# Eight shared-expert units in the attention stage's last slots, and three sum tables instead of two

## The chip, the cores and the metric

One Trainium2 chip, one of its cores. The metric is the time of the program on the device in microseconds (us). Engines: PE is TensorE (PEld its weight loads), DVE is VectorE, ACT is ScalarE, POOL is GpSimd, SP is SyncE, which issues most DMAs.

## What is computed

4096 tokens (16 sequences of 256, width 256) pass four layers, each `x = layernorm(x + layer(x))`: a recurrent attention (rwkv), a feed-forward layer on quantized weights (ffn), a latent attention with 16 heads (mla), and a mixture of experts (moe). The last one matters here:

```python
slots_token, slots_w = ...                    # router: 4 of 32 experts for each token, 160 places each
Xp = x[slots_token].reshape(E, C, d)
Y = (silu(Xp @ W_gate) * (Xp @ W_up)) @ W_down        # for each expert
out = zeros.at[slots_token].add(Y * slots_w)
shared = silu(x @ shared_gate.T) * (x @ shared_up.T) @ shared_down.T
return out + shared
```

## The kernel before

The four layers run one after another, each in its own block with a barrier at its end. In each block every engine has its own in-order list of instructions, written out by hand, and semaphores tie the lists together. Each fp32 operand of a matmul is split into a high part (ACT) and a low part (DVE, the source minus the high part), and each product is three matmuls (`PARTS`).

**Attention stage** (`attention_phase`). All engines walk over slots (seq, v), v = 0 to 11, for seq = 0 to NSEQ + 2 (NSEQ is 16). A sequence's scores are taken in its own slots; its projections run one and two sequences ahead; its last output projection is at (seq + 1, 8), its layer norm at (seq + 1, 9) and (seq + 1, 11); its routing in the slots of seq + 2 and the first two of seq + 3. Routing is a chain of 28 small steps, counted by the semaphore `chain`, that go back and forth between DVE (`route`, with times in `ROUTE_AT`), POOL (`route_pool`) and PE (transposes, logits, places). At its end POOL's `scatter` sends the rows of x, in eight indirect DMAs per sequence in slots 2 to 9 of seq + 3, to the table `slots` in DRAM. After (16, 3) no scores or sums are left: slots (16, 4) to (18, 11) hold only the last projection and the routing of sequences 14 and 15. SP stores x3 and loads x rows.

**Mixture stage** (`moe_phase`). SP loads expert weights and the table's rows (`e_rows`), eight experts ahead. For each expert e: PE transposes its rows (`expert_turn`), ACT and DVE split them and the weights, PE makes gate and up (`expert_in`), ACT takes silu, DVE the product, ACT and DVE split it, PE makes y (`expert_out`), ACT scales y into `y_rows` (`copy_y`), and POOL's `add_rows` adds it with two indirect accumulating DMAs of 80 rows into two tables in DRAM, `sums[0]` and `sums[1]`; each waits for the DMA before it on the same table. The shared expert works on 16 units of 256 tokens: `turn_x`, `shared_gate`, `shared_up`, `shared_out` on PE with their splits on ACT and DVE, and `add_shared` on DVE, which puts x + shared into `total`. One unit is made before the expert loop, one is spread over every three experts (`PACE`), and the last four come after the loop. Then the close: for each unit SP loads the two tables' rows (`load_sums`, after all scatters have landed, four units ahead), POOL adds the first (`add_first`), DVE adds the second and takes statistics (`combine`), POOL raises the variance to -1/2 (`rsqrt`), DVE makes the shift, ACT applies the norm and issues the store. The tables are zeroed in the ffn stage (`zero_tables`, one piece of each for each of its eight blocks).

## Time and profile before

| | us |
|---|---|
| median of 3 runs | 2151.86 (2151.37 to 2152.52) |
| the profiled execution, its time | 2142.46 |
| its span (first to last instruction) | 2140.6 |

The page of the profile gives busy time and instructions of each engine over the span, and the span in 40 equal slices (53.5 us each), a digit for tenths of a slice:

```profile
PE 1916.3 (90%) x12560; PEld 1707.8 (80%) x12560; DVE 1565.7 (73%) x4293; ACT 1049.0 (49%) x2674; POOL 844.8 (39%) x877
...
PE   6999999999999869995899999999999999739880
...
DVE  7978877788777635553578888888888888636547
ACT  5443333433333223331477666666666667326543
POOL 1222222323233200000244565665665555635556
PEclk9999999999999979996899999999999999869995
DMA  3200000000000043435100110000000000046756
```

Slices 1 to 14 are rwkv, 15 to 19 ffn, 20 to 35 the latent attention, the rest the mixture. PEclk is the clock that TensorE was granted, in tenths of full speed. The chain that ended last is followed back from the last instruction and takes at each step what released it:

```profile
DMA sums<-moe_y_rows,moe_e_rows 5%; DVE moe_stats L2458 1%; PE moe_up_ps L2503 1%; PE moe_down_ps L2524 0%; DVE moe_total L2454 0%; DVE moe_var_eps L2466 0%; PE moe_gate_ps L2503 0%; DVE moe_hidden L2373 0%; DVE moe_moments L2463 0%; ACT moe_h_high L2264 0%; PE moe_xt L2490 0%; DVE moe_h_low L2378 0%; DMA moe_e_rows<-slots 0%; DMA moe_x_rows<-x 0%; ACT moe_x_out L2347 0%
```

### The profile page before, as it was taken

What the parts mean: (1) busy time and instruction counts of PE and PEld (TensorE: products, weight loads), DVE (VectorE), ACT (ScalarE), POOL (GpSimd) and SP (SyncE); (2) the same over time, 40 slices, a digit from 0 to 9 for tenths busy, and PEclk for the clock granted to TensorE, in tenths of its full rate; (3) what the DMA queues carried; (4) which work ended last, traced back from release to release, by engine and by line L of the source; (5) the groups of instructions that cost most, each with busy time, mean ns of one, the idle gap of its engine ahead of it and who ended that gap; (6) DMA issues with size and microseconds to landing.
All of it is one profiled execution on the core that took longest, in us unless ns stands there. A gap on an engine that the chain in (4) does not pass through costs nothing. (4 is left out here: it accounts for less than half of the span.)

```text
span 2140.6 us, 36853 instructions
## 1 busy us (share of the span) xinstructions
PE 1916.3 (90%) x12560; PEld 1707.8 (80%) x12560; DVE 1565.7 (73%) x4293; ACT 1049.0 (49%) x2674; POOL 844.8 (39%) x877
## 2 busy tenths in 40 slices
PE   6999999999999869995899999999999999739880
PEld 5788888888888758884799889888888889639780
DVE  7978877788777635553578888888888888636547
ACT  5443333433333223331477666666666667326543
POOL 1222222323233200000244565665665555635556
PEclk9999999999999979996899999999999999869995
DMA  3200000000000043435100110000000000046756
GB/s 118 79 8 23 23 9 30 1 30 21 11 20 1 20 133 127 127 117 181 43 11 16 35 33 19 20 19 19 17 17 19 23 17 12 13 142 146 167 107 217
DMA packets 100619, 117.25 MB, mean 55 GB/s; under 512 B 12392, under 2 KB 92332, under 8 KB 99793
## 3 DMA queue, kind: packets, MB, share of 16 engines
q1 hardware_dynamic: 83792, 102.59, 15.1%
q0 software_dynamic: 12288, 8.11, 2.7%
q10 hardware_dynamic: 4352, 4.20, 0.7%
q8 instruction: 102, 1.67, 0.3%
q14 instruction: 85, 0.69, 0.1%
HBM read 75.42 MB, written 55.53 MB: 61 GB/s over the span
## 5 line engine op out<-in xcount | busy, mean ns | idle before, releaser
L212 POOL TENSOR_TENSOR rwkv_gate<-rwkv_key,rwkv_gate 128x512 f32<-128x512 f32 x128 | 203.6, 1590 | 529.4 <-DVE rwkv_key L408 529.4
L1196 POOL TENSOR_TENSOR mla_w_raw<-mla_w_raw,mla_row_inv 128x512 f32<-128x512 f32 x192 | 199.2, 1038 | 313.3 <-DVE mla_row_inv L1558 311.9
L1370 ACT ACTIVATE mla_w_raw<-mla_w_raw,mla_least 128x256 f32<-128x256 f32 (+1 forms) x512 | 227.8, 446 | 100.4 <-DVE mla_least L1542 99.3
L279 ACT ACTIVATE rwkv_gate<-rwkv_r 128x512 f32<-128x512 f32 x128 | 76.6, 598 | 403.9 <-DVE rwkv_o_low L332 400.8
L1542 DVE CUSTOM_DVE_ANT_0 mla_w_raw<-mla_score,mla_mask 128x256 f32<-128x256 f32 (+1 forms) x512 | 156.7, 352 | 81.4 <-PE mla_score L1881 81.2
L393 DVE TENSOR_TENSOR rwkv_kv<-rwkv_v,rwkv_key 128x512 f32<-128x512 f32 x128 | 88.0, 688 | 126.1 <-PE rwkv_v L441 123.8
L400 DVE TENSOR_TENSOR_SCAN rwkv_state<-rwkv_decay_w,rwkv_kv 128x256 f32<-128x256 f32 x256 | 166.1, 691 | 4.1
L1881 PE MATMUL mla_score<-mla_k_high,mla_q_high 128*128 128x256 f32 (+1 forms) x512 | 155.7, 304 | 0.0
L458 PE MATMUL rwkv_out<-rwkv_w_high,rwkv_o_high 128*128 128x256 f32 x512 | 142.2, 278 | 5.5 <-DVE rwkv_o_low L332 5.5
L1881 PE MATMUL mla_score<-mla_k_high,mla_q_low 128*128 128x256 f32 (+1 forms) x512 | 143.7, 281 | 0.0
L1881 PE MATMUL mla_score<-mla_k_low,mla_q_high 128*128 128x256 f32 (+1 forms) x512 | 143.2, 280 | 0.0
L458 PE MATMUL rwkv_out<-rwkv_w_low,rwkv_o_high 128*128 128x256 f32 x512 | 141.9, 277 | 0.0
L458 PE MATMUL rwkv_out<-rwkv_w_high,rwkv_o_low 128*128 128x256 f32 x512 | 141.9, 277 | 0.0
L1282 POOL DMA_INDIRECT slots<-mla_x_out,mla_slot_now x128 | 129.0, 1008 | 32.2 <-issue 22.2
L1386 ACT ACTIVATE mla_p_high<-mla_turn 128x512 fp32r<-128x512 f32 x192 | 114.0, 594 | 48.4 <-PE mla_turn L1890 48.3
L1552 DVE TENSOR_TENSOR mla_p_low<-mla_turn,mla_p_high 128x512 fp32r<-128x512 f32 x192 | 127.9, 666 | 0.5 <-ACT mla_p_high L1386 0.5
L2214 POOL DMA_INDIRECT sums<-moe_y_rows,moe_e_rows x64 | 92.7, 1448 | 87.3 <-DMA sums<-moe_y_rows,moe_e_rows 48.7
L1890 PE MATMUL mla_turn<-mla_ident,mla_w_raw 128*128 128x128 f32 x768 | 116.6, 274 | 11.3 <-DVE mla_p_low L1552 11.3
L1890 PEld LDWEIGHTS mla_turn<-mla_ident,mla_w_raw 128*128 128x128 f32 x768 | 91.4, 141 | 35.7 <-issue 22.5
L1909 PE MATMUL mla_o<-mla_p_high,mla_v_high 128*128 128x256 f32 x384 | 117.2, 305 | 0.7 <-DVE mla_o_low L1563 0.4
L1332 ACT ACTIVATE mla_q_high<-mla_turn 128x512 fp32r<-128x512 f32 x128 | 76.4, 599 | 68.4 <-PE mla_turn L1858 68.2
L1909 PE MATMUL mla_o<-mla_p_high,mla_v_low 128*128 128x256 f32 x384 | 107.9, 281 | 0.0
(372 smaller groups left out, 6464.8 us busy)
## 6 DMA issues: line engine op xcount, KB each, us to landing
moe_w_raw<-in_experts SPq DMA_DIRECT2D x32, 384.0 KB, 4.6
rwkv_w_raw<-in_rkvo SPq DMA_DIRECT2D x16, 512.0 KB, 3.3
moe_y_in<-sums SPq DMA_DIRECT2D x32, 256.0 KB, 3.4
sums<-ffn_empty SPq DMA_DIRECT2D x14, 512.0 KB, 7.7
slots<-ffn_empty SPq DMA_DIRECT2D x8, 722.5 KB, 6.4
moe_e_rows<-slots SPq DMA_DIRECT2D x32, 180.6 KB, 2.8
mla_w_raw<-in_mla_heads SPq DMA_DIRECT2D x4, 1280.0 KB, 7.2
rwkv_x_in<-in_x_t SPq DMA_DIRECT2D x16, 256.0 KB, 3.1
```

Source lines behind the costliest of these rows:

```text
L212: nc.gpsimd.tensor_tensor(gate[:, c % 2, :], key[:, c % 2, :], gate[:, c % 2, :], ALU.mult).then_inc(gated_done, 1)
L400: last_scan = nc.vector.tensor_tensor_scan(out=state[:, q, 1:SEQ + 1], data0=decay_w[:, c:c + 1].to_broadcast([P, SEQ]), data1=kv[:, q * S ...
L458: last = nc.tensor.matmul(out_ps[j // 2][:, (j % 2) * D:(j % 2 + 1) * D], o_part[op][:, c % 2, j * P:(j + 1) * P], w_part[wp][:, c, 3 * D: ...
L1196: nc.gpsimd.tensor_tensor(unit, unit, row_inv[:, v % PR, 0:len(heads)].rearrange("p (h a) -> p h a", a=1) .to_broadcast([P, len(heads), ke ...
L1282: nc.gpsimd.indirect_dma_start(slots_dram, bass.IndirectOffsetOnAxis(slot_now[:, of % 2, i:i + 1], 0), x_out[:, of % 2, i // TOPK, :], Non ...
L1370: last = nc.scalar.activation(probs[:, v % PR, i * keys:(i + 1) * keys], masked[:, v % 2, i * keys:(i + 1) * keys], ACT.Exp, bias=least[:, ...
L1386: nc.scalar.activation(p_part[0][:, v % PR, :], turn_ps[n % TURN_BANKS][:, :], ACT.Copy)\
L1542: last = nc.vector.tensor_tensor_reduce(out=masked[:, v % 2, i * keys:(i + 1) * keys], in0=score_ps[v % 2][:, i * keys:(i + 1) * keys], in ...
L1552: nc.vector.tensor_tensor(p_part[1][:, v % PR, :], turn_ps[n % TURN_BANKS][:, :], p_part[0][:, v % PR, :].bitcast(F32), ALU.subtract).then ...
L1881: last = nc.tensor.matmul(score_ps[v % 2][:, i * keys:(i + 1) * keys], q_part[qp][:, tile, h * P:(h + 1) * P], k_part[kp][:, par, 0:keys], ...
L1890: last = nc.tensor.transpose(ps[:, i * P:(i + 1) * P], probs[:, v % PR, i * P:(i + 1) * P], ident[:, :])
L1909: last = nc.tensor.matmul(out, v_part[vp][:, seq % 2, kb, b, :], probs_t, start=(i == 0), stop=(i == len(terms) - 1))
```

## The change

Units 0 to 7 of the shared expert (`EARLY`) are made in `attention_phase`, the other eight (`LATE`) in `moe_phase`, one ahead of the expert loop and one for every three of its first 21 experts; none is left for after the loop. The shared weights are loaded at slot (15, 0) into a part of `w_raw` that is free by then, and split in slots (15, 8) to (15, 10). The first unit is transposed at (16, 2); then the work is cut into 17 half steps, each at a slot of the list `TAIL`: an even one makes the gate product of its unit and the down product and add of the unit before, an odd one transposes the next unit and makes this one's up product and hidden values. They stand in each engine's list behind what that slot held before. PSUM banks and buffers of the scores, sums and projections are used for it. x + shared of these units is kept in `q_rows`, the split weights in `wq_high`; both buffers now outlive the stage.

There are three sum tables (`SUMS`): scatter number 2e + a goes into table (2e + a) % 3 and waits for the scatter three before. All three are zeroed in the ffn stage and loaded in the close, where DVE makes two adds instead of one.

```diff
-SUMS = 2
+SUMS = 3
...
+UT = 2
+UNIT = UT * P
+UNITS = TOKENS // UNIT
+XRING = 4
+WS = 3 * KD * SI
+EARLY = 8
+WS_SLOT = 8
+FIRST_X = (NSEQ, 2)
+TAIL = [(NSEQ + s, v) for s, v in ((0, 4), (0, 6), (0, 7), (0, 9), (0, 10), (1, 0), (1, 1), (1, 3), (1, 4), (1, 6),
+                                   (1, 7), (1, 9), (1, 10), (2, 0), (2, 2), (2, 4), (2, 6))]
...
+def kept_total(q_rows, u):
+
+    flat = q_rows[:, :, :, :].rearrange("p a h c -> p (a h c)")
+    return flat[:, u * UT * D:(u + 1) * UT * D].rearrange("p (t d) -> p t d", d=D)
...
+        shared_flat = w_raw[:, :, :, :].rearrange("p a h c -> p (a h c)")
+        ws_raw = shared_weights_of(shared_flat[:, 0:WS])
+        gate, hidden = (shared_flat[:, at:at + SC * UNIT].rearrange("p (c t) -> p c t", c=SC)
+                        for at in (WS, 2048))
+        sx_part = [wq_low[:, i * 1024:(i + 1) * 1024].rearrange("p (r k t) -> p r k t", r=2, k=KD) for i in range(2)]
+        sh_part = cq_part
+        ws_part = kept_weights(wq_high)
+        unit_x = [x_rows[:, :, :], cq_rows[:, :, :], x_res[:, 0, :, :], y_rows[:, 0, :, :]]
...
+            def load_shared():
+                sp.wait_ge(q_pe_done, 4 * NSEQ)
+                sp.dma_start(ws_raw.rearrange("p a k c -> p (a k c)"), w_shared).then_inc(ws_in, 16)
+
+            def load_unit(u):
+                if u == 0:
+                    sp.wait_ge(turn_filled, TURN_AT["x", 0, NSEQ - 1] + 1)
+                elif u == 1:
+                    sp.wait_ge(turn_filled, TURN_AT["cq", 0, NSEQ - 1] + 1)
+                elif u == 2:
+                    sp.wait_ge(res_added, 2 * (NSEQ - 1))
+                elif u == 3:
+                    sp.wait_ge(normed, NSEQ - 1)
+                else:
+                    sp.wait_ge(total_done, u - XRING + 1)
+                sp.dma_start(unit_x[u % XRING], seq_rows(x3, u)).then_inc(unit_in[u % XRING], 16)
+
...
+                if (seq, v) == (NSEQ - 1, 0):
+                    sp.wait_ge(stored, 16 * (NSEQ - 3))
+                    load_shared()
                 if v == 0 and exists(seq - 2):
                     store(seq - 2)
+                if (seq, v) == (NSEQ - 1, 0):
+                    load_unit(0)
+                    load_unit(1)
+                if (seq, v) == (NSEQ, 0):
+                    load_unit(2)
+                    load_unit(3)
+                half = half_step(seq, v)
+                if half is not None and half % 2 == 0 and half >= 2 and half // 2 - 1 + XRING < EARLY:
+                    load_unit(half // 2 - 1 + XRING)
...
@@ -1435,6 +1518,42 @@
                     exps(seq, v)
                 if v == 6 and exists(seq + 1):
                     values_high(seq + 1, 1 - par)
+                if seq == NSEQ - 1 and 0 <= v - WS_SLOT < 3:
+                    shared_weights(v - WS_SLOT)
+                if (seq, v) == FIRST_X:
+                    unit_high(0)
+                half = half_step(seq, v)
+                if half is not None and half % 2 == 0 and half // 2 < EARLY:
+                    unit_gate(half // 2)
+                elif half is not None and half % 2 == 1:
+                    if half // 2 + 1 < EARLY:
+                        unit_high(half // 2 + 1)
+                    unit_hidden_high(half // 2)
+
...
+            def unit_gate(u):
+                act.wait_ge(gate_ready, u + 1)
+                if u >= 1:
+                    act.wait_ge(hidden_done, u)
+                nc.scalar.activation(gate, score_ps[0][:, :].rearrange("p (c t) -> p c t", c=SC), ACT.Silu)\
+                    .then_inc(gate_done, 1)
...
+                if seq == NSEQ - 1 and 0 <= v - WS_SLOT < 3:
+                    shared_weights(v - WS_SLOT)
+                if (seq, v) == FIRST_X:
+                    unit_low(0)
+                half = half_step(seq, v)
+                if half is not None and half % 2 == 0 and half >= 2:
+                    add_shared(half // 2 - 1)
+                elif half is not None and half % 2 == 1:
+                    if half // 2 + 1 < EARLY:
+                        unit_low(half // 2 + 1)
+                    unit_hidden(half // 2)
+                    unit_hidden_low(half // 2)
+
...
+            def unit_low(u):
+                dve.wait_ge(sx_high, u + 1)
+                nc.vector.tensor_tensor(sx_part[1][:, u % 2, :, :], proj_ps[:, :].rearrange("p (k t) -> p k t", k=KD),
+                                        sx_part[0][:, u % 2, :, :].bitcast(F32), ALU.subtract).then_inc(sx_low, 1)
...
+            def unit_hidden(u):
+                dve.wait_ge(up_ready, u + 1)
+                dve.wait_ge(gate_done, u + 1)
+                if u >= 1:
+                    dve.wait_ge(sh_low, u)
+                nc.vector.tensor_tensor(hidden, score_ps[1][:, :].rearrange("p (c t) -> p c t", c=SC), gate, ALU.mult)\
+                    .then_inc(hidden_done, 1)
+
+            def unit_hidden_low(u):
+                dve.wait_ge(sh_high, u + 1)
+                nc.vector.tensor_tensor(sh_part[1][:, :, :], hidden, sh_part[0][:, :, :].bitcast(F32),
+                                        ALU.subtract).then_inc(sh_low, 1)
+
+            def add_shared(u):
+                dve.wait_ge(shared_done, u + 1)
+                dve.wait_ge(unit_in[u % XRING], 16 * (u // XRING + 1))
+                nc.vector.tensor_tensor(kept_total(q_rows, u), o_ps[0][:, :].rearrange("p (t d) -> p t d", d=D),
+                                        unit_x[u % XRING], ALU.add).then_inc(total_done, 1)
...
+                if (seq, v) == FIRST_X:
+                    turn_unit(0)
+                half = half_step(seq, v)
+                if half is not None and half % 2 == 0:
+                    if half // 2 < EARLY:
+                        unit_in_matmul(half // 2, 0, score_ps[0], gate_ready, gate_done)
+                    if half >= 2:
+                        unit_out(half // 2 - 1)
+                elif half is not None:
+                    if half // 2 + 1 < EARLY:
+                        turn_unit(half // 2 + 1)
+                    unit_in_matmul(half // 2, 1, score_ps[1], up_ready, hidden_done)
+
+            def turn_unit(u):
+                if u == 0:
+                    pe.wait_ge(q_turned, 4 * NSEQ)
+                    pe.wait_ge(q_abs_done, 4 * NSEQ)
+                else:
+                    pe.wait_ge(sx_low, u)
+                pe.wait_ge(unit_in[u % XRING], 16 * (u // XRING + 1))
+                for k in range(KD):
+                    for j in range(UT):
+                        last = nc.tensor.transpose(proj_ps[:, k * UNIT + j * P:k * UNIT + (j + 1) * P],
+                                                   unit_x[u % XRING][:, j, k * P:(k + 1) * P], ident[:, :])
+                last.then_inc(transposed, 1)
+
+            def unit_in_matmul(u, b, bank, ready, read):
+                pe.wait_ge(sx_low, u + 1)
+                if u == 0:
+                    pe.wait_ge(ws_low, b + 1)
+                    pe.wait_ge(masked_done, SLOTS * NSEQ)
+                else:
+                    pe.wait_ge(read, u)
+                for c in range(SC):
+                    for i, (wp, xp) in enumerate(PARTS):
+                        for k in range(KD):
+                            last = nc.tensor.matmul(bank[:, c * UNIT:(c + 1) * UNIT],
+                                                    ws_part[wp][:, b, k, c * P:(c + 1) * P],
+                                                    sx_part[xp][:, u % 2, k, :],
+                                                    start=(i == 0 and k == 0), stop=(i == 2 and k == KD - 1))
+                last.then_inc(ready, 1)
+
+            def unit_out(u):
+                pe.wait_ge(sh_low, u + 1)
+                if u == 0:
+                    pe.wait_ge(ws_low, 3)
+                    pe.wait_ge(o_low, 8 * NSEQ)
+                else:
+                    pe.wait_ge(total_done, u)
+                for j in range(UT):
+                    for c in range(SC):
+                        for i, (hp, wp) in enumerate(PARTS):
+                            last = nc.tensor.matmul(o_ps[0][:, j * D:(j + 1) * D],
+                                                    sh_part[hp][:, c, j * P:(j + 1) * P], ws_part[wp][:, 2, c, :],
+                                                    start=(c == 0 and i == 0), stop=(c == SC - 1 and i == 2))
+                last.then_inc(shared_done, 1)
...
-                if piece == 0 and u - 1 + XRING < UNITS:
+                if piece == 0 and u - 1 + XRING < LATE:
...
-                    if e >= 1:
-                        pool.wait_ge(y_added[(e - 1) % RING][a], 16 * ((e - 1) // RING + 1))
+                    if 2 * e + a >= SUMS:
+                        e1, a1 = divmod(2 * e + a - SUMS, 2)
+                        pool.wait_ge(y_added[e1 % RING][a1], 16 * (e1 // RING + 1))
                     nc.gpsimd.indirect_dma_start(
-                        sums_dram[a],
+                        sums_dram[(2 * e + a) % SUMS],
                         bass.IndirectOffsetOnAxis(e_rows[:, e % RING, a, IDCOL:ROW].bitcast(U32), 0),
...
-                pool.wait_ge(total_done, n + 1)
+                if n >= EARLY:
+                    pool.wait_ge(total_done, n - EARLY + 1)
...
                 dve.wait_ge(first_added, n + 1)
-                nc.vector.tensor_tensor(tiles(n), y_in[:, n % SUMRING, 1, :, :], tiles(n), ALU.add)\
-                    .then_inc(all_added, 1)
-                dve.wait_ge(all_added, n + 1)
+                for a in range(1, SUMS):
+                    nc.vector.tensor_tensor(tiles(n), y_in[:, n % SUMRING, a, :, :], tiles(n), ALU.add)\
+                        .then_inc(all_added, 1)
+                    dve.wait_ge(all_added, (SUMS - 1) * n + a)
                 for t in range(UT):
-                    nc.vector.bn_stats(stats[:, n % 2, t, :], total[:, UT * n + t, :]).then_inc(counted, 1)
+                    nc.vector.bn_stats(stats[:, n % 2, t, :], tiles(n)[:, t, :]).then_inc(counted, 1)
...
                     turn_x(u + 1)
-                if piece == 2:
+                if piece == 2 and u < LATE:
                     shared_out(u)
                 expert_out(e)
 
-            for u in range(HEAD + INNER, UNITS):
-                shared_gate(u)
-                shared_out(u - 1)
-                if u + 1 < UNITS:
-                    turn_x(u + 1)
-                shared_up(u)
-            shared_out(UNITS - 1)
```

## Rows read from the trace of the kernel before

**Rows 1.** Busy time by stage: PE, PEld, DVE, ACT, POOL with counts, PEclk, DMA share, GB/s.
```profile
1856.00:1900.60 44.60, 4.49 (x26) 3.78 (x26) 11.47 (x60) 0.82 (x2) 24.79 (x39) 0.53 0.03 8
1923.00:1966.00 43.00, 42.09 (x373) 41.12 (x372) 29.36 (x57) 30.87 (x74) 23.08 (x16) 1.00 0.64 156
...
2094.00:2134.00 40.00, 0.00 (x0) 0.00 (x0) 36.69 (x112) 15.81 (x30) 35.47 (x30) 0.54 0.80 247
```

**Rows 2.** Timelines of POOL and DVE, attention tail: start, us, engine line op.
```profile
1868.91 1.04 POOL L1282 DMA_INDIRECT slots<-mla_x_out,mla_slot_now  x1 [3.40 <-DVE mla_slot_now L1681]
...
1887.06 0.99 POOL L1282 DMA_INDIRECT slots<-mla_x_out,mla_slot_now  x1 [1.84 <-DVE mla_slot_now L1681]
...
1855.97 0.42 DVE L1573 TENSOR_TENSOR mla_y_rows<-mla_turn,mla_x_res 128x256 f32<-128x256 f32 x1
```

**Rows 3.** Waits of 1904 to 2066; time to landing of the scatters (L2214).
```profile
POOL sums L2214 <- DMA sums<-moe_y_rows,moe_e_rows: 44.7, 26, 3.2
...
DMA to landing us min/median/max: 3.1/3.6/5.9
```

**Rows 4.** Timeline of POOL, the accumulating scatters of the expert stage.
```profile
1923.51 2.18 POOL L2214 DMA_INDIRECT sums<-moe_y_rows,moe_e_rows  x1 [22.73 <-ACT moe_y_rows L2299]
...
1929.03 1.40 POOL L2214 DMA_INDIRECT sums<-moe_y_rows,moe_e_rows  x1 [1.60 <-DMA sums<-moe_y_rows,moe_e_rows]
...
2074.73 1.40 POOL L2214 DMA_INDIRECT sums<-moe_y_rows,moe_e_rows  x1 [0.90 <-DMA sums<-moe_y_rows,moe_e_rows]
...
2079.07 1.68 POOL L2214 DMA_INDIRECT sums<-moe_y_rows,moe_e_rows  x1 [1.20 <-DMA sums<-moe_y_rows,moe_e_rows]
```

**Rows 5.** Chain of work, one leftover unit: start us, us, what.
```profile
2081.24 0.44 PE moe_xt L2490 x4
2081.67 1.45 PE moe_up_ps L2503 x12
...
2083.14 0.70 DVE moe_hidden L2373
...
2083.87 0.64 ACT moe_h_high L2264
...
2084.53 0.70 DVE moe_h_low L2378
...
2085.28 1.70 PE moe_down_ps L2524 x12
```

**Rows 6.** Chain of work, start of the expert stage.
```profile
1905.79 1.05 ACT moe_ws_high L2244
1906.86 1.24 DVE moe_ws_low L2360
```

**Rows 7.** Timeline of ACT, copies of y, six experts apart.
```profile
1933.97 0.81 ACT L2299 ACTIVATE moe_y_rows<-moe_y,moe_e_rows 80x256 f32<-80x256 f32 x2
...
1958.12 0.81 ACT L2299 ACTIVATE moe_y_rows<-moe_y,moe_e_rows 80x256 f32<-80x256 f32 x2
```

**Rows 8.** Busy time by stage (columns of rows 1), the close with DMA full.
```profile
2100.00:2124.00 24.00, 0.00 (x0) 0.00 (x0) 22.32 (x69) 9.96 (x19) 22.95 (x20) 0.50 1.01 313
```

**Rows 9.** Timelines of DVE and POOL in the close.
```profile
2128.16 0.65 DVE L2466 TENSOR_SCALAR moe_var_eps<-moe_moments 128x2 f32<-128x2 f32 x1
...
2133.20 0.17 DVE L2466 TENSOR_SCALAR moe_var_eps<-moe_moments 128x2 f32<-128x2 f32 x1
...
2086.18 1.29 POOL L2226 TENSOR_TENSOR moe_total<-moe_y_in,moe_total 128x512 f32<-128x512 f32 x1 [5.42 <-DMA moe_y_in<-sums]
...
2128.88 1.18 POOL L2231 TENSOR_TENSOR moe_rstd<-moe_var_eps,moe_minus_half 128x2 f32<-128x2 f32 x1
2130.04 1.26 POOL L2226 TENSOR_TENSOR moe_total<-moe_y_in,moe_total 128x512 f32<-128x512 f32 x1
...
2133.45 0.69 POOL L2231 TENSOR_TENSOR moe_rstd<-moe_var_eps,moe_minus_half 128x2 f32<-128x2 f32 x1 [0.86 <-DVE moe_var_eps L2466]
```

More of the change, by code:

```diff
@@ L2185, in _ @@
                     load_slots(e - 1 + RING)
-            for u in range(HEAD + INNER - 1 + XRING, UNITS):
-                load_x(u)
             def load_sums(n):
@@ L2319, in _ @@
                     copy_y(e - 1)
-                if piece == 2:
+                if piece == 2 and u + 1 < LATE:
                     x_high(u + 1)
@@ L2431, in _ @@
                     weights_low(e + 2)
[L2432 removed]
+                if piece == 1 and u < LATE:
                     shared_hidden(u)
@@ L2435, in _ @@
                     rows_low(e + 2)
-                if piece == 2:
+                if piece == 2 and u + 1 < LATE:
                     x_low(u + 1)
```

142 lines of the change are left out of this document (69 added, 73 removed).

## The prediction, made before the result was known

> **What bounds the kernel now.** I read the stages first [rows 1], then the waits, then the chain. Three stages matter. From 1856 to 1900.6 the attention stage has no scores left: TensorE is busy 4.5 us of 44.6, VectorE 11.5, GpSimd 24.8. Only the routing of the last two sequences runs, a ping-pong of small VectorE and GpSimd steps with two groups of eight scatters; the last group, which starts at 1887.06, sets the end [rows 2]. In the expert stage TensorE is full at first (42.1 of 43), with e_rows loaded ahead. What ends last over the whole stage is the accumulate into the sums tables: each of the two tables takes one transfer at a time, and GpSimd waits 44.7 us for its own transfers; these land a median of 3.6 us after issue [rows 3]. The 64 scatters run from 1923.51 to 2079.07, 31 steps from expert to expert at 5.0 us [rows 4]. Four leftover shared units run at its end, each one chain of engines, and the closing stage (16 units of add, statistics, norm) starts only at 2094. There VectorE and GpSimd are both over 88% busy [rows 1].
>
> **Change part 1, units in the attention tail.** Eight units are added as 17 half steps between slots (16,4) and (18,6). One unit by itself is a chain [rows 5]: transposes 0.44, up 1.45, hidden product 0.70, its high part 0.64, its low part 0.70, out 1.70, which repeats in 5.75 us with gaps. These same instructions, with VectorE's x low part and the add (0.70 each, from their like in the chain), now stand in the in-order queues between routing steps. An odd half step holds VectorE from its x low part to the hidden low part (0.7 + 0.7 + 0.64 waiting for ScalarE + 0.7, near 2.8, more where the up product isn't there yet); an even one holds it until TensorE's out product is there, then 0.7. I walked the slots with these durations and the recorded gaps of the routing steps. Slot (16,2) delays the logits' reading by 1.4. In (16,7) TensorE has gate and out of units 0 and 1 ahead of sequence 15's last projection, whose residual add was at 1855.97 [rows 2] and now comes at 1864.2: +8.2. One stretch shows the walk: out of unit 1 ends 1870.95, its add 1871.65, routing steps 20 to 22 and the norm of sequence 15 1873.0; TensorE transposes the routed rows until 1873.5, unit 3 until 1873.95, makes up of unit 2 until 1875.4; VectorE ends the x low part 1875.3, the hidden product 1876.1, ScalarE its high part 1876.8, VectorE the low part 1877.5, and only behind these come the routed rows' high part (1877.4) and low part (1878.2), and steps 25 to 28 of sequence 14 (1879.2). So the scatters of sequence 14 start 0.8 later, at 1880.0 instead of 1868.91: +11.1. From there to sequence 15's scatters the old time is 18.15; in it now stand four more odd and four more even half steps, some 23 us of chain, of which 15 falls into gaps where VectorE waited for GpSimd, and 8.3 does not. So the last scatters start at 1906.4 instead of 1887.06: +19.4. Units 6 and 7 end under those scatters (1911.7 against some 1916). Bounds: 0 if all falls into VectorE's 33 idle us [rows 1]; 46, eight chains of 5.75, if none does. The walk is nearest to what is issued, so I take 19.4. Queued behind the new waits are: on TensorE the last projection, the routed transposes, the logits and both place counts; on ScalarE the routed high part and the exponentials; on VectorE all routing; and GpSimd waits for that. SP gets the weights' load, four x loads and later four more, ahead of two stores and a residual load that have a whole sequence of slack: nothing. The weights' splits (three of about 0.7 on VectorE) go into sequence 15, where VectorE has some slack and TensorE little: between 0 and 2, I take 0.5.
>
> **Part 2, the expert stage's head.** The shared weights' splits (1.05 and 1.24) were in the chain [rows 6] and go: -2.3. Their 0.79 MB also leave the crowded DMA start; between -1 and -5.
>
> **Part 3, experts.** Before 1966, with e_rows preloaded, the expert loop already ran at its own pace: y copies of six experts from 1933.97 to 1958.12, 4.03 us each, TensorE full [rows 7, 1]. A third table lets three transfers be open. On one table issue to issue took 5.5 us at the start, with DMA full (1923.51 to 1929.03), and 4.3 at the end (2074.73 to 2079.07) [rows 4]; with three tables two scatters need two thirds of that, 2.9 to 3.7. GpSimd itself needs 2 x (1.40 + 0.30 between two issues) = 3.4, with its longer ones 3.5. That is under 4.03, so the 21 experts that still carry a unit go at TensorE's pace: 21 x 4.03 = 84.6. The other ten have no unit: TensorE and ScalarE (30.9 busy of 43 with units [rows 1], so under 3.3 without, waits included) are faster than GpSimd, hence 10 x 3.5 = 35. With the second scatter 1.75 and its landing 3.3 the stage from first scatter to last landing is 124.7, against 2079.07 + 3.3 - 1923.51 = 158.9: -34.2. What is late next is TensorE, then GpSimd's issue. Bounds for the pace: 3.9 and 4.4 with a unit, 3.3 and 4.3 without (one table's step at the old end): -40 to -19.
>
> **Part 4, the close.** Before, 58.2 us from last landing (2082.4) to the end, 11 of them waiting for leftover units. Now the first load of three tables starts at the landing: 3.8 as before (2082.4 to the add at 2086.18 [rows 9]), 0.8 for the third table at 313 GB/s [rows 8], 1.3 for the first add, 5.9 in all. The pace per unit was 2.5 (39.4 us for 16). The rows show what it is made of [rows 9]: VectorE's var_eps takes 0.65 where GpSimd's add runs beside it and 0.17 where none does; GpSimd's power takes 1.18 beside VectorE's add and 0.69 alone. So they don't overlap: 1.26 + 0.59 (the power while the add doesn't hold it) + 0.65 is the whole pace. One more VectorE add of 0.69 and its gap, if it fits behind the power, makes 3.28; 16 x 3.28 = 52.5, then 7.4 from the last var_eps to the end as before: 65.8, +7.6. DMA must give 1.05 MB in 3.28 us, 320 GB/s; rows 8 show 313 at a full share, so up to 2 more.
>
> The Trainium skill ("SBUF — State Buffer", Who interferes with whom) says that a VectorE instruction with two SBUF inputs and a GpSimd instruction that reads SBUF exclude each other for their whole length, by order of issue. By this rule, too, the added add is paid in full and not hidden, and the trace agrees (0.65 against 0.17). It does not say who goes first when both wait.
>
> **Part 5, zeroing a third table.** Eight more writes of 512 KB, 1.7 us each at 313 GB/s, on SP ahead of each store. The layer runs on TensorE there and DMA is at 0 to 5 tenths in the page's slices. From 0 to 2; I take 0.
>
> **Sum.** 19.4 + 0.5 - 2.3 - 34.2 + 7.6 + 0 = -9.0 on the profiled execution's 2142.46 (span 2140.6), so 2133.5. The timed median, 2151.86, lies 9.4 above that execution; I carry the difference over: 2142.9.
>
> **Rivals.** *A, the close is taken in the wrong order.* After VectorE's first add, GpSimd's power (0.6) and then directly its next add (1.26) may run before VectorE's second add. Then the unit is 0.65 + 0.6 + 1.26 + 0.65 + statistics 1.0 + var_eps 0.2 = 4.4: 16 x 1.17 more, +19, giving 2162, slower than before. It decides from the point where VectorE is passed over in more than half of the units. For it: GpSimd's two instructions follow each other without a gap [rows 9]. Against: VectorE waits longer and would be first in line. *B, TensorE's clock falls.* In 1856 to 1900.6 the granted clock was 0.53 with little work [rows 1]. With units TensorE is some 85% busy, in the ten unitless experts about 70%. If it stays at its lower level, transposes, up and out double, 3.6 us on each unit's chain: with four to five units in that state +16, 2159. Against: the leftover units' chain, 5.3 busy in 5.75, ran at these short times. *C, the third table buys nothing,* because transfers wait for each other in the DMA engines: pace stays 5.0, -34.2 becomes 0 to -10, and the time is 2168 or more. Against: two tables' transfers do overlap, and a scatter of 80 rows lands in 3.1 at best, most of it not data. *D, the routing hides more:* half the 19.4, giving 2133. It is for this that TensorE and ScalarE were idle; against it stands that VectorE's queue is in order.
>
> The Trainium skill ("DMA: Bandwidth & Descriptors", Anatomy of one DMA) puts about 2.0 us of a transfer down to a fixed part, mostly the receipt of the last write. By this rule open transfers overlap and C fails; by estimate from it, three tables could go at 2/3 of the old table time, 3.3, no bound beside GpSimd. The landing of 3.1 at best agrees.
>
> **How the numbers follow.** Forecast as summed 50%, A 20%, B 12%, C 6%, D 12%. Around 2143 the forecast's own range is 2134 to 2153 (tail 12 to 26, experts -40 to -28, close +5 to +12). About 0.2%, 4.3 us, is what a measurement of this kernel tells from no change. The forecast gives faster 0.37, same 0.10, slower 0.03; D faster 0.12; A 0.02, 0.05, 0.13; B 0, 0.05, 0.07; C slower 0.06: faster 0.51, same 0.20, slower 0.29. Eight in ten lie from 2131 to 2163: below it is D with a quick expert stage, above it C and the worst of A and B.
>
> **What would show it.** Last slot scatters starting near 1906, expert stage starting near 1920; y copies 4.0 apart for 21 experts, then 3.5 with GpSimd without waits for sums; 125 us from first scatter to last landing; closing units every 3.3 us with var_eps still stretched. Wrong would be: a last scatter at 1897 or 1920, a clock of 0.5 between 1860 and 1900, gaps of 5 between experts, closing units every 4.4.

## The result, and the profile after

| | before | changed | ratio, 95% interval |
|---|---|---|---|
| median, us | 2152.19 (2151.37 to 2158.70) | 2130.96 (2128.49 to 2135.95) | 0.990, 0.987 to 0.992 |
| profiled execution (span) | 2142.46 (2140.6) | 2135.95 (2134.2) | |
| both again, changed kernel a second time | 2150.13 | 2133.63 | 0.992, 0.990 to 0.995 |
| both again, a third time | 2149.02 | 2135.19 | 0.993, 0.991 to 0.996 |

The change makes the kernel faster, by 21 us in the first comparison, 17 and 14 in the repeats. I had forecast 9, and 2142.9 with a range from 2131 to 2163. The direction was right, the size not: 2130.96 lies at the very edge of the range.

The page of the changed kernel: busy time, the 40 slices (53.4 us each), and its chain that ended last.

```profile
PE 1916.8 (90%) x12560; PEld 1709.6 (80%) x12560; DVE 1568.0 (73%) x4310; ACT 1050.0 (49%) x2677; POOL 848.7 (40%) x877
...
POOL 1232323222232200000144556666655566643767
PEclk9999999999999979997899999999999999998985
DMA  3200000010000044445100010000000000107768
...
DMA sums<-moe_y_rows,moe_e_rows 1%; PE moe_gate_ps L2672 1%; PE moe_y L2728 1%; PE moe_eup L2717 1%; PE moe_egate L2717 1%; PE moe_up_ps L2672 1%; DVE moe_stats L2629 1%; DVE kept_q_rows L2625 0%; DVE moe_total L2625 0%; PE moe_down_ps L2691 0%; PE moe_et L2703 0%; DVE moe_w_low L2570 0%; DMA moe_y_in<-sums 0%; DVE moe_moments L2634 0%; DVE moe_e_low L2575 0%
```

Busy times hardly moved, since no work was added but a third add per closing unit. The chain did: the wait for the sums tables' transfers falls from 5% to 1% of the span, and TensorE's expert and shared products stand in its place.

GpSimd's timeline (start, length, what it waited for) has the stage borders: first slot scatters of sequences 14 and 15, start of the expert stage, first and last two scatters into the sums, first add of the close. It answers [rows 2, 4].

```profile
1887.44 1.04 POOL L1365 DMA_INDIRECT slots<-mla_x_out,mla_slot_now  x1 [7.73 <-DVE mla_slot_now L1800]
1912.44 0.99 POOL L1365 DMA_INDIRECT slots<-mla_x_out,mla_slot_now  x1 [3.98 <-DVE mla_slot_now L1800]
1926.21 0.10 POOL L2402 MEMSET moe_minus_half<- 128x2 f32 x1 [3.85 <-POOLq L62]
1947.59 2.17 POOL L2411 DMA_INDIRECT sums<-moe_y_rows,moe_e_rows  x1 [21.28 <-ACT moe_y_rows L2493]
...
2071.71 1.40 POOL L2411 DMA_INDIRECT sums<-moe_y_rows,moe_e_rows  x1 [0.30 <-DMA sums<-moe_y_rows,moe_e_rows]
2073.42 1.40 POOL L2411 DMA_INDIRECT sums<-moe_y_rows,moe_e_rows  x1 [0.30 <-issue]
2082.07 1.26 POOL L2424 TENSOR_TENSOR kept_q_rows<-moe_y_in,kept_q_rows 128x512 f32<-128x512 f32 x1 [7.25 <-DMA moe_y_in<-sums]
```

At the end scatters follow each other every 1.71 us (1.40 and a gap of 0.30): GpSimd itself is the limit there. Over the whole loop its waits (us in total, times, longest) are as follows. The 44.7 for transfers in [rows 3] end at 2066; the whole loop of the kernel before has 48.7.

```profile
POOL sums L2411 <- ACT moe_y_rows L2493: 22.5, 4, 21.3
POOL sums L2411 <- DMA sums<-moe_y_rows,moe_e_rows: 21.1, 27, 2.7
POOL sums L2411 <- issue: 10.5, 33, 0.6
```

Both kernels were run three times with a profile, so each stage can be read three times. "Drift" below is what the stage start has moved by ahead of the added units. Times from here on, such as the "loop" (first to last scatter into the sums) and the "rest" (last scatter to the end), are of profiled executions; medians are of all executions of a run.

| stage, us | before (three executions) | changed (three) | difference of means | forecast |
|---|---|---|---|---|
| expert stage starts at | 1900.7, 1902.9, 1908.9 | 1926.2, 1928.7, 1928.6 | +23.7, some 3 of it drift | +19.9 |
| its start to first sums scatter | 22.8, 22.7, 23.8 | 21.4, 21.5, 20.8 | -1.9 | -2.3 |
| first to last sums scatter | 155.6, 159.9, 158.0 | 125.8, 120.7, 123.2 | -34.6 | -34.2 |
| last scatter to end | 61.5, 58.2, 58.4 | 60.8, 60.9, 61.5 | +1.7 | +7.6 |
| span | 2140.6, 2143.7, 2149.0 | 2134.2, 2131.8, 2134.1 | -11.0 | -9.0 |

### The profile page after: what moved, and what is told of

It is laid out like the page before. It is cut to its first block and busy times, and to the rows that moved or that the text cites. A ratio compares the mean times of both kernels' runs of the same rounds, so it can differ in the third digit from the quotient of the medians.

```text
span 2134.2 us, 36884 instructions
## 1 busy us (share of the span) xinstructions
PE 1916.8 (90%) x12560; PEld 1709.6 (80%) x12560; DVE 1568.0 (73%) x4310; ACT 1050.0 (49%) x2677; POOL 848.7 (40%) x877
## 5 line engine op out<-in xcount | busy, mean ns | idle before, releaser
L393 DVE TENSOR_TENSOR rwkv_kv<-rwkv_v,rwkv_key 128x512 f32<-128x512 f32 x128 | 88.0, 688 | 125.8 <-PE rwkv_v L441 122.3
L1469 ACT ACTIVATE mla_p_high<-mla_turn 128x512 fp32r<-128x512 f32 x192 | 114.0, 594 | 48.7 <-PE mla_turn L2050 48.4
```

What stands on the lines that cost most here:

```text
L1469: nc.scalar.activation(p_part[0][:, v % PR, :], turn_ps[n % TURN_BANKS][:, :], ACT.Copy)\
```

## Experiments

Ratios are to the kernel before, run beside each.

**Where single executions differ: both kernels again.** No edit.

> The kernel before, unchanged, for a second profiled execution. My sum stood on an execution of 2142.46 us while the timed ones lie at 2152. Theory 1 (that execution was an odd one): the new profiled execution lies within 2 us of 2152, and the 9 us more stand in the expert stage, where the first-to-last scatter takes 160 to 165 us instead of 155.6. Theory 2 (a profiled execution is always quicker than a timed one): it is near 2142 again, with 155.6 there.

> The kernel before, for a third profiled execution. Theory 1 (something in kernels with two tables makes the profiled execution 7 to 9 us quicker than the timed ones): it lies again 7 to 9 below the median of its timed runs. Theory 2 (chance: three such executions happened to have few falls of the clock and a quick loop): anywhere within 5 of the median.

> The changed kernel once more, beside the three below. Single executions of the kernel before lie from 2136 to 2161 us. Theory 1: an execution loses 2.7 us each time TensorE's granted clock falls to 0.5 for some 6.5 us inside the attention layer (the profiled one had two such falls, the kernel before one), so that the true gain is 15 to 21 us: median 2130 to 2134 where the kernel before has 2147 to 2152. Theory 2 (the first comparison was the exact one): ratio 0.990, 21 less than before.

> The changed kernel, for a third profiled execution and a direct comparison with the mixed version. Both theories: ratio to the kernel before 0.990 to 0.992, profiled execution within 5 of the median, last slot scatters of sequence 15 some 21 us later than in the kernel before once falls of the clock (2.7 each) are taken off.

Profiled executions of the kernel before took 2142.5, 2145.5 and 2150.8; timed ones between 2136 and 2161. The third lies on its median (2150.0). Chance, then: no rule puts profiled executions of two tables ahead.

These runs also say how much a comparison can tell. Set beside itself, the kernel before had 2153.1 against 2147.2, ratio 1.002 (1.000 to 1.004), in the first run and 2150.0 against 2149.0, ratio 0.999 (0.997 to 1.001), in the second. So two medians of one kernel can lie 6 us apart, and an interval that just misses 1 shows nothing here. One execution of the third table alone took 3396 us and one of the changed kernel's third set 6952; why is not known, and the medians hardly feel them.

Part of what varies is seen in windows over one attention sequence each (length, busy time of PE, PEld, DVE, ACT, POOL with counts, granted clock, DMA share, GB/s), here the changed kernel's first execution:

```profile
1499.80:1550.90 51.10, 49.18 (x381) 45.72 (x380) 43.55 (x179) 34.64 (x113) 30.87 (x40) 1.00 0.06 18
1550.90:1604.70 53.80, 52.02 (x381) 48.72 (x380) 43.63 (x179) 34.71 (x113) 30.82 (x39) 0.94 0.06 17
```

The same 381 matmuls take 51.1 us, or 53.8 when the mean clock is 0.94. Inside the slow one:

```profile
1554.00:1555.00 1.00, 0.16 (x2) 0.17 (x2) 1.00 (x4) 1.00 (x5) 0.79 (x1) 0.99 0.00 0
1555.00:1556.00 1.00, 1.00 (x7) 1.00 (x6) 0.97 (x4) 0.87 (x4) 0.25 (x1) 0.50 0.00 0
...
1560.00:1562.00 2.00, 2.00 (x7) 1.48 (x6) 1.32 (x4) 1.84 (x9) 1.00 (x2) 0.55 0.00 0
1562.00:1564.00 2.00, 2.00 (x21) 2.00 (x20) 0.62 (x2) 1.09 (x2) 0.00 (x0) 1.00 0.04 8
```

TensorE stands still for most of one microsecond at the head of this sequence and of the one before it, and in some sequences its clock falls right behind that from its upper level (2.4 GHz) to the lower one (1.2 GHz) for some 6 to 7 us of full work, which costs 2.7. The sequence before this one has the pause (0.23 busy in 1503 to 1504) and no fall. The kernel before had one such fall in its first and second executions, two and two short ones of 1.1 us in its third; the changed kernel two in each, and a short one in its third; early units with two tables none in one execution and two in the other. So part of the drift of 3 in the table is falls; where the rest arises was not traced, and whether the changed kernel draws more falls was not settled. The timed executions have no trace, so how much of their spread is falls isn't shown.

**The third table alone**, in the kernel before.

```diff
-SUMS = 2
+SUMS = 3
...
-                    if e >= 1:
-                        pool.wait_ge(y_added[(e - 1) % RING][a], 16 * ((e - 1) // RING + 1))
+                    if 2 * e + a >= SUMS:
+                        e1, a1 = divmod(2 * e + a - SUMS, 2)
+                        pool.wait_ge(y_added[e1 % RING][a1], 16 * (e1 // RING + 1))
...
-                        sums_dram[a],
+                        sums_dram[(2 * e + a) % SUMS],
```

> The kernel before with the third sums table alone; all sixteen shared units stay where they were. Theory 1 (the parts add): 31 steps at TensorE's 4.03 us give 125 us from first to last scatter instead of 155.6, the four units behind the loop stay, the close gets 3 to 6 longer: 2152 - 31 + 5 = 2126, ahead of the changed kernel's 2131. Theory 2 (the tables help only where units are gone from the expert loop, since TensorE is the bound there): 140 us for the scatters and 2140 in all.

> The kernel before with the third table alone, once more beside these. Theory 1 (early units give nothing on top of the tables): ratio 0.992 to 0.993, as the changed kernel's. Theory 2 (they give what the first comparisons suggest): 0.994 or more.

2131.8 and 2130.9; ratios 0.993 (0.990 to 0.995) and 0.994 (0.992 to 0.996). The changed kernel has 2131 to 2135, and the spans of the profiled executions are 2124.9 and 2130.7 here against its 2131.8 to 2134.2. So nearly all of the gain is the third table's; what the early units add on top of it, up to 6 us either way, is not settled. First to last scatter took 126.0 and 128.4: Theory 1 of the loop was right. In its first 40 us from the first scatter, and in the next 40, TensorE is full:

```profile
1923.70:1963.70 40.00, 39.89 (x355) 39.04 (x354) 27.66 (x54) 28.95 (x71) 29.62 (x20) 1.00 0.84 204
1963.70:2003.70 40.00, 39.85 (x351) 38.77 (x349) 27.02 (x53) 28.29 (x70) 27.03 (x20) 1.00 0.85 210
```

The rest was 9 to 12 us off: last scatter to end took 75.2 and 72.7, 14.5 more than before, and I had put 3 to 6 on it. The loop now ends ahead of the leftover units: VectorE's first closing add starts at 2073.91, behind the last unit's add, when GpSimd's first add had long started, at 2058.19.

**The early units alone**, the changed kernel with two tables.

```diff
-SUMS = 3
+SUMS = 2
```

> The changed kernel with two sums tables: early units alone. Theory 1 (the parts add, expert loop bound by the two tables): the attention tail costs +20, the head of the expert stage gives -1.4, the loop stays at 155, the four leftover units' wait of 11 goes: 2152 + 20 - 1 - 11 = 2160, slower than the kernel before. Theory 2 (fewer units in the loop shorten it by themselves, by ten or more): 2150 or less.

> Early units with two tables, once more. Theory 1 (two tables): the profiled execution lies 7 to 9 below the median again, ratio to the kernel before 1.001 to 1.005. Theory 2 (chance): the same ratio, profiled execution within 5 of the median.

2152.5 and 2152.9; ratios 1.003 (1.001 to 1.005) twice. The kernel before against itself gave 1.002, so this is no gain, and a loss of 4 to 7 us at most. Both theories were half right. The tail pays +18 to +20; the loop took 147.9 and 146.5 (about 11 less than before, although there were still two tables), last scatter to end 55.4 and 55.3 (4 less). The second profiled execution, 2153.15, lies on its median.

This run and the changed kernel differ in the table alone, and so give its price in the close: closing units every 2.52 us here and every 2.73 there, 3 us over the stage, where I had forecast 3.28. The stage is 5.7 longer in all; 2 of that is the longer wait for the first loads (8.6 to 9.3 us behind the last scatter instead of 6.9).

**The closing add left out.**

```diff
-                for a in range(1, SUMS):
+                for a in range(1, SUMS - 1):
...
-                    dve.wait_ge(all_added, (SUMS - 1) * n + a)
+                    dve.wait_ge(all_added, (SUMS - 2) * n + a)
```

> The changed kernel, where the closing stage loads the third table and does not add it (so a third of the expert sums is left out of the result). Theory 1 (VectorE's second add mostly fills time in which it waited): the closing pace falls from 2.73 to about 2.5 us a unit, 16 x 0.2 = 3 to 4 less in all, 2127. Theory 2 (as in my prediction, the add is paid in full, 0.69 and a gap a unit): 11 less, 2120.

2134.1, ratio 0.993 (0.991 to 0.996), no less than the changed kernel's. Last scatter to end is 59.0 against 61.1. The pace is 2.52 for seven units, the same as with two tables, and then 2.7 to 3.0, since the three tables' loads don't come faster: GpSimd waits six times for them.

```profile
POOL moe_total L2424 <- DMA moe_y_in<-sums: 1.9, 6, 0.5
```

With one VectorE add, VectorE's var_eps is stretched again, as before the change:

```profile
2093.82 1.26 POOL L2424 TENSOR_TENSOR kept_q_rows<-moe_y_in,kept_q_rows 128x512 f32<-128x512 f32 x1
...
2094.46 0.65 DVE L2637 TENSOR_SCALAR moe_var_eps<-moe_moments 128x2 f32<-128x2 f32 x1
```

So leaving the add out is worth 2 us (3 if the loads kept up), not the 11 of Theory 2. Where it goes is seen in one closing unit of the changed kernel, VectorE and GpSimd:

```profile
2102.11 0.17 DVE L2637 TENSOR_SCALAR moe_var_eps<-moe_moments 128x2 f32<-128x2 f32 x1
2102.19 0.15 DVE L2642 SCALAR_TENSOR_TENSOR moe_shift<-moe_moments,moe_rstd 128x2 f32<-128x2 f32 x1
2102.26 1.41 DVE L2625 TENSOR_TENSOR kept_q_rows<-moe_y_in,kept_q_rows 128x512 f32<-128x512 f32 x2
2102.36 1.15 POOL L2429 TENSOR_TENSOR moe_rstd<-moe_var_eps,moe_minus_half 128x2 f32<-128x2 f32 x1 [0.30 <-DVE moe_var_eps L2637]
...
2103.49 1.31 POOL L2424 TENSOR_TENSOR moe_total<-moe_y_in,moe_total 128x512 f32<-128x512 f32 x1
...
2103.71 0.75 DVE L2629 BATCH_NORM_STATS2 moe_stats<-kept_q_rows 128x6 f32<-128x256 f32 x2
2104.56 0.25 DVE L2634 BATCH_NORM_AGGREGATE moe_moments<-moe_stats 128x2 f32<-128x6 f32 x2
2104.84 0.17 DVE L2637 TENSOR_SCALAR moe_var_eps<-moe_moments 128x2 f32<-128x2 f32 x1
```

VectorE's own work is the pace: 1.41 + 0.75 + 0.25 + 0.17 + 0.15 = 2.73 (the 1.41 is both adds). GpSimd's power is still stretched by the first add (1.15; it takes 0.70 in the kernel with one table below, whose close has no VectorE add), but its last 0.56, to 2103.51, runs beside the second add, 2102.95 to 2103.67. GpSimd's add starts at 2103.49, when the second add is nearly through; and var_eps, which it used to stretch to 0.65 [rows 9], comes after it has ended and takes 0.17.

**A fourth table.**

```diff
-SUMS = 3
+SUMS = 4
```

> The changed kernel with four sums tables. It had 21 us in which GpSimd waited for its own transfers. Theory 1: that wait falls to under 6; the loop goes from 126 to about 119 (21 experts at 4.03, ten at 3.4), and the close pays VectorE's third add in full, since VectorE is its bound now: 2.73 to 3.4 us a unit, +11; in all +4, 2135. Theory 2 (the loop is bound by the DMA engines or TensorE): it stays at 125 and the sum is +11 or more, 2142.

2155.9, ratio 1.003 (1.001 to 1.005). The loop took 120.4, and GpSimd waited hardly at all for its transfers:

```profile
POOL sums L2411 <- DMA sums<-moe_y_rows,moe_e_rows: 1.9, 6, 0.4
```

But the close has a pace of 4.43, a loss of 1.70 a unit where Theory 1 had 0.67:

```profile
2107.58 3.11 DVE L2625 TENSOR_TENSOR kept_q_rows<-moe_y_in,kept_q_rows 128x512 f32<-128x512 f32 x3
2107.68 1.15 POOL L2429 TENSOR_TENSOR moe_rstd<-moe_var_eps,moe_minus_half 128x2 f32<-128x2 f32 x1 [1.98 <-DVE moe_var_eps L2637]
...
2108.80 1.34 POOL L2424 TENSOR_TENSOR kept_q_rows<-moe_y_in,kept_q_rows 128x512 f32<-128x512 f32 x1
```

Three adds take 2.14 in the first two closing units; here they take 3.11. The third comes when GpSimd's add has begun (2108.80) and ends 0.55 behind its end (2110.14). This is the order of my rival A, with its price (4.4), but it needs a third VectorE add; with two, both are through. The Trainium skill ("SBUF — State Buffer", Who interferes with whom) calls the ports that VectorE and GpSimd share an exclusive lock, and says of VectorE's two-port modes that whoever issues first holds them for its whole instruction. I had carried "whole instruction" over to adds with two SBUF inputs, of which the page says only that they contend with a GpSimd instruction that reads SBUF. The add of 3.11 agrees with that reading, the 0.56 of the power beside a VectorE add does not: only part of that GpSimd instruction's time excludes the add.

**One table.**

> The changed kernel with a single sums table, so that each of the 64 scatters waits for the landing of the one before. It is a test of where the 17 to 21 us of the timed runs come from, when the profiled executions differ by 6 to 9 only: with two tables the profiled execution was 7 to 9 us below the median (three kernels), with three or more within 5 either way. Theory 1 (a landing takes some 0.2 to 0.3 us less in a profiled execution than in a timed one): here, with 64 landings in a row, the profiled execution is 12 to 20 us below the median of the timed ones. Theory 2 (chance, or falls of the clock): within 5 us, either way. Time itself: 64 x 4.5 = 290 for the loop, about 2290.

```diff
-SUMS = 3
+SUMS = 1
```

2268.2, ratio 1.057 (1.055 to 1.060); the profiled execution took 2266.0, 2 below the median. Theory 2: by this, landings don't differ between profiled and timed executions by more than some 0.03 us each. The loop took 272.5, a scatter each 4.3 us; I had put 4.5 on one. This close has no VectorE add, and shows what GpSimd's power takes by itself:

```profile
2236.91 0.70 POOL L2429 TENSOR_TENSOR moe_rstd<-moe_var_eps,moe_minus_half 128x2 f32<-128x2 f32 x1
```

**Fewer early units, early and late slots.** Five units in 11 half steps; eleven in the expert stage.

```diff
-EARLY = 8
+EARLY = 5
...
-TAIL = [(NSEQ + s, v) for s, v in ((0, 4), (0, 6), (0, 7), (0, 9), (0, 10), (1, 0), (1, 1), (1, 3), (1, 4), (1, 6),
-                                   (1, 7), (1, 9), (1, 10), (2, 0), (2, 2), (2, 4), (2, 6))]
+TAIL = [(NSEQ + s, v) for s, v in ((0, 10), (1, 0), (1, 1), (1, 3), (1, 6), (1, 9), (2, 0), (2, 2), (2, 4), (2, 6),
+                                   (2, 8))]
```

> Three sums tables and five early units instead of eight, in the first 11 of the 17 slots of the list; the expert stage has eleven units, one for each three experts up to the last ones. Theory 1 (the tail is paid by half step, the loop is bound by GpSimd and its own transfers and hides the three units that come back): the tail costs 12 to 15 instead of 20, the loop stays at 126, the close stays as it is: 5 to 8 less than the changed kernel, 2125. Theory 2 (the loop is bound by TensorE): it gets 3 to 4 longer and the gain is 2 to 4.

> The same with the 11 half steps later: none before the last output projection at (16,8), the last four beside the last group of slot scatters. Theory 1 (my walk: 8 of the 11 us by which the scatters of sequence 14 slip come from gate and out products ahead of the last projection, and half steps beside the last scatters are free): the tail costs 5 to 9, last scatters of the slots start near 1893 instead of 1887, 2118 in all. Theory 2 (each half step costs the same wherever it stands): 12 to 15, as with the early slots.

2129.0 and 2129.4, ratios 0.990 (0.988 to 0.992) and 0.990 (0.988 to 0.993), beside the changed kernel's 2133.6; the loops took 125.6 and 127.3. A measure of the tail without drift is from GpSimd's norm step of sequence 14 (the last ahead of all half steps) to the first slot scatter of sequence 15. It was 46.1 before, 66.4, 66.4 and 65.1 in the changed kernel, 60.4 with five units in the early slots and 57.4 in the late ones. So the early slots cost 14.3, within the 12 to 15 of Theory 1, though the whole gained 4.6 where that theory had 5 to 8; the late ones cost 11.2, more than the 5 to 9 of their Theory 1, less than the 12 to 15 of Theory 2.

**Four or three, spaced.** Nine slots, two to four apart, the last four beside the last scatters; the last unit of the expert stage is finished behind the loop. For three units the slots are (17,1), (17,4), (17,10), (18,2), (18,4), (18,6), (18,8), and one unit stands wholly behind the loop.

```diff
-EARLY = 8
+EARLY = 4
...
+TAIL = [(NSEQ + s, v) for s, v in ((0, 10), (1, 1), (1, 4), (1, 7), (1, 10), (2, 2), (2, 4), (2, 6), (2, 8))]
...
+            for u in range(12, LATE):
+                shared_gate(u)
+                shared_out(u - 1)
+                ...
+            shared_out(LATE - 1)
```

> Three tables, four early units in nine late slots, the other twelve in the expert stage, the last of which is finished behind the loop. Theory 1 (a unit costs the tail 2.6 us wherever its half steps stand, and a unit that ends less than 8 us behind the last scatter costs nothing, because the close waits for landing and load anyway): tail +10 instead of 21, loop and close unchanged, 2122. Theory 2 (a part of the tail's cost is there as soon as one unit is): 2127, as with five.

> The same with three early units and one unit wholly behind the loop. Theory 1: tail +7, the unit behind the loop and the rest of the one before it fit under the 8 us of landing and load but for some 2: 2121. Theory 2 (each unit behind the loop costs 3.6, as four of them cost 14 with tables alone): 2125.

> Three tables, four early units, once more. Theory 1 (it saves the tail's share of four units, some 10 us, against the changed kernel, and the loop and the close stay): 6 to 11 us less than the changed kernel on the same chip, ratio to the kernel before 0.986 to 0.988. Theory 2 (2121.8 came from a quick chip): 2 to 5 less than the changed kernel, ratio 0.989.

Four units: 2121.8 and, beside the changed kernel, 2120.6 against its 2135.2; ratios 0.989 (0.988 to 0.991) and 0.988 (0.985 to 0.990). It beats both kernels, the changed one by 14.5 us, more than Theory 1 had. Three units: 2122.2, 0.989, the same. The tail measure is 48.7 and 47.2 with four, 48.5 with three; the loop 126.7 and 125.9, the rest 60.8 and 60.4. Four units cost the tail 1 to 3 us, and 0.7 behind the last scatters; eight cost 20.

**Number or slots?** The four units in the first nine slots of the changed kernel's list.

```diff
+TAIL = [(NSEQ + s, v) for s, v in ((0, 4), (0, 6), (0, 7), (0, 9), (0, 10), (1, 0), (1, 1), (1, 3), (1, 4))]
```

> The four early units of the mixed version in the first nine of the changed kernel's slots, (16,4) to (17,4), instead of nine slots three apart of which four stand beside the last scatters. In the mixed version the routing of sequence 15 (last norm of sequence 14 to first scatter of sequence 15) took 47 to 49 us where the kernel before needs 46 and the changed kernel 66. Theory 1 (the slots decide: half steps one and two slots apart find their own chain unfinished and hold VectorE): 57 to 60 us, and 9 to 12 more in all than the mixed version, 2131. Theory 2 (the number of half steps decides, and four units are few enough to hide): 50 or less, and within 3 of the mixed version.

2130.8, ratio 0.991 (0.989 to 0.993), and the tail measure 60.4, as Theory 1 said. It is the slots, and not the number of units. The spaced list differs from this one in two things, though: its half steps lie farther apart, and its last four stand beside the last scatters, behind the stretch that is measured. Which of the two saves how much was not tested. Windows over that stretch, first of the kernel before:

```profile
1840.90:1887.10 46.20, 17.03 (x130) 15.29 (x128) 22.73 (x102) 5.95 (x15) 26.64 (x47) 0.69 0.05 14
```

The changed kernel:

```profile
1846.00:1912.40 66.40, 54.84 (x420) 51.30 (x419) 40.43 (x131) 23.29 (x42) 26.91 (x46) 0.95 0.12 34
```

Four units, spaced:

```profile
1846.20:1894.90 48.70, 32.23 (x236) 30.59 (x235) 29.53 (x114) 14.93 (x28) 26.98 (x47) 0.86 0.09 24
```

Four units in the dense list:

```profile
1847.80:1908.20 60.40, 37.63 (x283) 34.97 (x281) 33.38 (x119) 15.25 (x30) 26.56 (x45) 0.83 0.07 19
```

With four spaced units TensorE is busy 32 of 49 us and GpSimd stays at 27, as in all four. With the dense list 4 to 5 us more of TensorE's and VectorE's work is done in that stretch, and it gets 12 longer. Where it goes stands in VectorE's waits there, in the changed kernel:

```profile
DVE kept_q_rows L1909 <- PE mla_o L2210: 7.7, 6, 1.7
DVE mla_cq_low L1903 <- ACT mla_cq_high L1556: 4.2, 6, 0.7
DVE mla_wq_low L1890 <- ACT mla_wq_low L1542: 2.6, 2, 1.9
```

And with four spaced units:

```profile
DVE mla_cq_low L1902 <- ACT mla_cq_high L1555: 1.4, 2, 0.7
...
DVE kept_q_rows L1908 <- issue: 1.1, 1, 1.1
DVE mla_wq_low L1889 <- ACT mla_wq_low L1541: 0.7, 1, 0.7
```

Close together, an add meets its own out product unfinished and holds VectorE, and routing behind it, 7.7 us in six waits (6.1 in four with the dense four); spaced, VectorE has no such wait. The three waits of the changed kernel's list add up to 14.5 us, and the kernel before has none of them; its VectorE waited 15.7 us there for GpSimd's routing steps, and little of that is left.

## Why the prediction was right or wrong

- **Tail, +19.4: right.** The drift-free measure says +20.3, +20.3 and +19.0. The last scatters start at 1912.44, 1907 without the 5.1 that had come before any half step; I had 1906.4. Its two halves were each 1 to 2 us off, the other way round: sequence 14's scatters slipped by 13.4 and sequence 15's by 7 more; I had 11.1 and 8.3. Holding VectorE until the chain of the half step is there was the mechanism, as VectorE's waits above show. Rival D, more hidden, is false for these slots and true for spaced ones, which I had not looked at.
- **Weights' splits, +0.5: about right.** The norm of sequence 14 comes 0.8 later behind that of 13 in the changed kernel.
- **Head, -2.3: right**, -1.9.
- **Experts, -34.2: right.** Means of three executions give -34.6 (mine included the last landing, which hardly moved); the single pair on which I would have judged gives -29.7. The copies of y come 4.02 us apart over most experts with a unit and 3.45 apart behind them; I had 4.03 and 3.5. "GpSimd without waits for sums" holds only for the last experts: over the loop it still waits 14 to 21 us for transfers, which the fourth table takes away for 3 us of loop.
- **The close, +7.6: the step that failed.** "So they don't overlap: 1.26 + 0.59 ... + 0.65 is the whole pace. One more VectorE add ... makes 3.28". The pace is 2.73, and the stage changed by +1.7. I read the power's stretch beside an add as one block of work that excludes the add, and kept var_eps at 0.65 beside GpSimd's add. What the runs show in its place: the power's last 0.56 runs beside the second add, and with that add in the way var_eps falls behind GpSimd's add and is 0.17 again. VectorE, not the sum of both engines, sets the pace. With 16 units the pace alone is 16 x 0.55 = 9 us too high. The whole term comes out 8 too high against the execution that I had forecast from (its stage took 61.5, I forecast 69.1, the mean is 61.1), and 6 against the mean of three, since the other two executions before had 58.2 and 58.4. Two runs show it: two tables have 2.52 and three 2.73 with everything else the same, and var_eps is back at 0.65 with the second add left out.
- **Rival A, +19: false for three tables, true for four.** (Its own sum gives 4.36 a unit and so 17, not 19.) Rival C is false. Rival B, the clock, too: it was 0.95 in the tail and 1.00 for most of the loop.
- **The sum and the median.** Profiled executions differ by 11.0 in their means, against 9.0. That this looks near is luck: the close was 6 too high, and the start of the expert stage came 4 later than forecast, 3 of it drift that no unit made. With the close as it is my sum would have been -15, and the comparisons gave -21, -17 and -14. The first rests on four executions of each kernel. What it has beyond -15 is no more than the 6 us by which two medians of the kernel before differed, so that it needs no further cause, though none is excluded; the 0.2% that I had said a measurement can tell was too small. The offset of 9.4 which I carried over was chance: the third profiled execution lies on its median. Carrying it was harmless here, since it was in the before's time as well. How the microseconds between -11 and -15 to -17 fall on the stages isn't settled: executions of one kernel vary by 2 to 8 us, and a stage by up to 5.
- **What neither sum said:** the parts aren't additive. Tables alone give -13 to -15, units alone +4 to +7, both -14 to -21. On top of the tables, units take 20 in the tail and give back 13 in the close, where with three tables the leftover units had come late, and 4 in the loop.

## What to carry to other kernels

When work is moved into an idle stretch of in-order queues, cost it by where each step stands, not by total: a step of a chain should be placed where its input is already there, or beside work that it doesn't delay. Here four units cost 1 to 3 us in one list of slots and 14 in another, and eight cost 20. A small saving at the front of a loop may uncover work behind it, so price each part with the other in place. And before reading a gain of a few microseconds, compare the unchanged kernel with itself: here that alone gave 6 us once, and executions lay up to 5 us apart in a single stage.

## What the hardware showed that I had not expected

- TensorE's clock fell from 1.00 to 0.50 for 6 to 7 us inside stretches of 49.2 us work in 51.1, right behind a pause in which TensorE was busy 0.16 of a microsecond, in none to four of the sixteen sequences of an execution, at 2.7 us each (1.1 for a short one).
- GpSimd's power on 128x2 elements takes 0.69 alone and 1.15 beside a VectorE add: it ends 0.56 behind the add that was there first, and that 0.56 runs beside the next one. GpSimd's add on 128x512 (1.26 to 1.34) does hold a later VectorE add back: the third of four tables' adds ends 0.55 behind it.
- Loading three tables (768 KB a closing unit, beside a store of 256 KB) comes every 2.7 to 3.0 us in the later half of the close: with the second add left out, GpSimd waited for its loads there.
